# Local attention without values: probabilities times the layer's input, value and output weights folded on the chip

## The reference

```python
def attn_layer(x, Wqkv, qs, ksc, Wo):            # 16 heads of 64
    q, k, v = jnp.split(x @ Wqkv, 3, -1)          # each reshaped to (b, heads, n, 64)
    q = l2norm(q) * qs;  k = l2norm(k) * ksc
    q, k = rotary(q), rotary(k)
    out = local_attention(q, k, v)                # windows of 32 queries, 64 keys: own and previous window
    return out.reshape(b, n, 1024) @ Wo

for i in range(6):
    x = attn_layer(shift_tokens(x), Wqkv[i], q_scale[i], k_scale[i], Wo[i]) + x
    x = ffn_layer(shift_tokens(x), ln_g[i], ln_b[i], W1[i], b1[i], W2[i], b2[i]) + x
```

## Time and profile before

| | |
|---|---|
| time, median of 3 runs | 4451.77 us (4450.44 to 4455.33) |
| time of the profiled execution | 4455.55 us |
| its span | 4454.2 us |
| the last phase in it (from about 1399 us) | some 3055 us |
| one layer (2562 to 3065 us) | 503 us; PE busy 495.2, ACT 414.7, DVE 401.5, POOL 364.6 |
| PE busy over the span | 3995.9 us (90%) |
| chain that ended last, by engine | PE 72%, issue 8%, DVE 7%, POOL 6%, ACT 5% |
| DMA engines' mean busy share in the last phase | 0.25 |
| issues: 128 KB transfers, 64 KB transfers, 63.5 KB, 0.2 KB | 768, 864, 96, 96 |

### The profile page before, as it was taken

The page is one execution under the profiler, slowest core; times in us unless marked ns, Lnnn a source line. Parts: engine busy times, 40 slices in busy tenths (PEclk is TensorE's granted clock), DMA queues, the critical chain, the costliest instruction groups (busy, mean ns, idle before and its releaser), DMA issues.

```text
span 4454.2 us, 182201 instructions
## 1 busy us (share of the span) xinstructions
PE 3995.9 (90%) x79168; PEld 2929.8 (66%) x79168; DVE 3362.1 (75%) x6090; ACT 3370.5 (76%) x5129; POOL 2877.6 (65%) x2623
## 2 busy tenths in 40 slices
PE   7888456666887999999999999999999999999998
PEld 5666345455664667777777767777777767777777
DVE  4665898983555878787888877787888877887875
ACT  4665788884454878888888888887888888888886
POOL 1111788882435877776777777777777777777774
PEclk9999787878998999999999999999999999999999
DMA  2000000000000222222222222222222222222222
GB/s 63 2 2 2 1 1 1 1 1 28 2 2 8 61 66 57 70 64 56 64 67 66 62 61 59 71 62 57 62 59 73 63 58 60 70 66 56 62 56 64
DMA packets 173226, 201.21 MB, mean 45 GB/s; under 512 B 82256, under 2 KB 93712, under 8 KB 172304
## 3 DMA queue, kind: packets, MB, share of 16 engines
q1 hardware_dynamic: 172432, 189.56, 16.8%
HBM read 23.79 MB, written 2.10 MB: 6 GB/s over the span
## 4 chain that ended last, share of the span: by engine, by line
PE 72%; issue 8%; DVE 7%; POOL 6%; ACT 5%; DMA 0%; POOLq 0%; DVEq 0%; ACTq 0%; SPq 0%
PE ps L1331 8%; PE ps L1267 8%; PE ps L1340 7%; PE ps L1268 7%; PE ps L1297 6%; PE ps L1276 5%; PE ps L1315 4%; PE ps L1316 3%; PE ps L1370 3%; PE ps L1364 3%; PE ps L1381 3%; PE ps L1308 2%; DVE arena L616 2%; PE ps L362 2%; PE ps L1287 1%
## 5 line engine op out<-in xcount | busy, mean ns | idle before, releaser
L1605 POOL TENSOR_TENSOR arena<-arena 128x1024 f32<-128x1024 f32 x384 | 722.9, 1904 | 346.9 <-ACT arena L1415 346.9
L1599 POOL TENSOR_TENSOR arena<-arena 128x1024 f32<-128x1024 f32 x384 | 902.1, 2371 | 7.2 <-DVE arena L1507 7.2
L1506 DVE TENSOR_TENSOR arena<-ps,arena 128x1024 f32<-128x1024 f32 x384 | 466.7, 1215 | 189.4 <-ACT arena L1399 183.1
L1618 POOL TENSOR_TENSOR arena<-arena 128x1024 f32<-128x1024 f32 x192 | 365.5, 1904 | 310.3 <-DVE arena L1535 310.3
L1331 PEld LDWEIGHTS ps<-arena 64*64 64x64 f32 x24576 | 381.3, 135 | 166.4 <-issue 165.8
L226 POOL TENSOR_SCALAR arena<-arena 128x2 f32<-128x2 f32 x256 | 73.9, 288 | 611.7 <-DVE arena L220 600.6
L1507 DVE TENSOR_TENSOR arena<-ps,arena 128x1024 f32<-128x1024 f32 x384 | 465.8, 1213 | 0.0
L1515 DVE TENSOR_REDUCE arena<-arena 128x32 f32<-128x2048 f32 x192 | 437.8, 2280 | 0.7 <-issue 0.7
L1267 PE MATMUL ps<-arena 128*128 128x512 f32 x768 | 427.8, 639 | 5.6 <-DVE arena L1507 2.8
L1340 PEld LDWEIGHTS ps<-arena 128*128 128x128 f32 x3072 | 373.0, 192 | 90.4 <-issue 90.1
L1331 PE MATMUL ps<-arena 64*64 64x32 f32 x24576 | 406.1, 220 | 19.9 <-issue 18.9
(11 more groups left out here) (252 smaller groups left out, 9460.6 us busy)
## 6 DMA issues: line engine op xcount, KB each, us to landing
arena<-arena SPq DMA_DIRECT2D x768, 128.0 KB
arena<-arena SPq DMA_DIRECT2D x864, 64.0 KB
arena<-in_dWqkv SPq DMA_DIRECT2D x18, 512.0 KB, 4.9
arena<-arena SPq DMA_DIRECT2D x96, 63.5 KB
arena<-in_dWo SPq DMA_DIRECT2D x6, 512.0 KB
arena<-in_x SPq DMA_DIRECT2D x4, 512.0 KB, 7.5
out<-arena SPq DMA_DIRECT2D x8, 256.0 KB, 2.3
arena<-in_dW SPq DMA_DIRECT2D x6, 341.0 KB, 2.9
```

The lines of the kernel that those rows point to most:

```text
L1506: dve.tensor_tensor(o1, p.rearrange("p (h e) -> p h e", h=16), bc(cs, 1, 16), ALU.mult)
L1599: pool.tensor_tensor(a1[:, half], a1[:, half], T2[:, half], ALU.add).then_inc(*radd[g].up())
L1605: pool.tensor_tensor(a3, a3, bc(ss[:, 16 * g:16 * g + 16], 2, 64), ALU.mult).then_inc(*nrm[g].up())
```

## The change

By associativity, probabilities x (x Wv) x Wo = (probabilities x x) x (Wv Wo). The change computes the product of value and output weights per head on the chip, once a layer (pieces `wv0`, `wv1` on TensorE, `we0`, `we1` on ScalarE, result WVO), and multiplies the probabilities of every head by the layer's shifted input itself:

- Gone per tile: `v`, `vn`, `vd` (8 transfers), `o`, `oT`.
- New per batch: `xd`, 22 transfers on SP out of XX into XW (two buffers), the stretches of the input that the windows need. xd of batch m waits, among others, for u0 and u1 of tile 2m-3, the last readers of its buffer.
- New per tile: `u0` and `u1` (4 matmuls of 64 rows x 128 outputs x 256 columns each, the two row halves into different PSUM banks), `uT0`, `uT1` (two copies of 128 x 1024). u0, u1 wait for xd of their batch.
- `wo` has 16 steps of 128 x 128 in place of 8, and waits for both uT.
- The table of numbers is another one, so all pieces stand in a new order, and PSUM slots are handed out anew; the weights' loads change accordingly (wvT and wo for the next layer early, at 8000). XS has three buffers in place of four.

```diff
-    TILE = {"q1": 999, "q0": 1401, ..., "o": 7478, "oT": 8280, "wo": 9611, "xxa": 10157}
-    BATCH = {"sh": 0, "xs": 598, "fd": 12837, "fst": 15069, "frs": 17286, "fn": 18737, ...
+    TILE = {..., "ex": 7311, "pn": 7674, "sum": 7840, "PT": 8499,
+            "p": 8653, "uT1": 8779, "u1": 8911, "uT0": 9719, "u0": 9883, "xxa": 10114, "wo": 10515}
+    BATCH = {"xs": 0, "sh": 362, "xd": 6011, "fd": 12295, "frs": 12295, "fst": 12701, "fn": 18195, ...
...
-            if piece == "o":
...
+            if piece in ("u0", "u1"):
+                g = int(piece[1])
                 pe.wait_ge(*S.PT.at(n + 1))
+                pe.wait_ge(*xw[m % 2].at(352 * (m // 2 + 1)))
+                p, pT, w = claim(piece, n), PT[n % 2].rearrange("p (g c b q) -> p g c b q", g=2, c=8, b=2), XW[m % 2]
+                for blk in range(2):
+                    for u in range(2):
+                        half = slice(64 * u, 64 * u + 64)
+                        i = pe.matmul(p[:, 512 * u:512 * u + 512].rearrange("p (c b q) -> p c b q", c=8, b=2)[:, :, blk, :],
+                                      w[half, k % 2, 2 * g + blk, :], pT[half, g, :, blk, :], start=True, stop=True,
+                                      skip_group_check=True)
+                i.then_inc(*u_ps[g].up())
             if piece == "wo":
...
+                for u in range(2):
+                    for c in range(8):
+                        i = pe.matmul(p[:, 0:128], o[:, u, c, :], w[:, u, c, :], start=(u == c == 0), stop=(u == 1 and c == 7))
...
-            if piece == "vd":
...
+            if piece == "xd":
+                m = l * NB + k
+                if m == 0:
+                    sp.wait_ge(*S.zeroed.at(1))
+                if l:
+                    sp.wait_ge(*S.xxf.at(m - NB + 1))
+                if m >= 2:
+                    sp.wait_ge(*S.u0_ps.at(2 * m - 2))
+                    sp.wait_ge(*S.u1_ps.at(2 * m - 2))
+                x, got = XX[:, 2 * k:2 * k + 2, :], xw[m % 2]
+                for u in range(2):
+                    w = XW[m % 2][64 * u:64 * u + 64]
+                    sp.dma_start(w[0:32, 1, 0, 0:64], x[96:128, 0, 0:64]).then_inc(*got.dma())
+                    sp.dma_start(w[0:33, 1, 0, 64:128], x[95:128, 0, 64:128]).then_inc(*got.dma())
+                    sp.dma_start(w[0:1, 1, 1, 64:128], x[127:128, 0, 64:128]).then_inc(*got.dma())
+                    sp.dma_start(w[32:64, :, 0, 0:64], x[0:32, :, 0:64]).then_inc(*got.dma())
+                    sp.dma_start(w[33:64, :, 0, 64:128], x[0:31, :, 64:128]).then_inc(*got.dma())
...
```

More of the change, by code:

```diff
@@ L1213, in phase_d @@
     PP = [sb([128, 16, 64]) for _ in range(3)]
-    VN = [sb([128, 1024]) for _ in range(3)]
-    VW = [sb([128, 3, 512]) for _ in range(2)]
+    XW = [sb([128, 2, 4, 128]) for _ in range(2)]
+    WVO = [sb([128, 2, 8, 128]) for _ in range(2)]
     PT = [sb([128, 1024]) for _ in range(2)]
-    OT = [sb([128, 8, 128]) for _ in range(2)]
+    UT = [sb([128, 2, 8, 128]) for _ in range(2)]
     SM = [sb([128, 3, 16]) for _ in range(3)]
     FB = [(stats(C), sb([128, 2]), sb([128, 2, 128]), sb([128, 2, 128]), sb([128, 3, 256])) for _ in range(NF)]
-    TILE = {"q1": 999, "q0": 1401, "sq1": 1620, "ro1": 1906, "ro0": 1925, "sq0": 1965, "ssum": 2373, "radd1": 2611,
[3 rows of a table removed]
[L1225 to L1228, removed]
+    TILE = {"sq1": 1943, "ro1": 2031, "ro0": 2073, "sq0": 2108, "q1": 2140, "q0": 2147, "radd1": 2171, "radd0": 2343,
[3 rows of a table added]
+    BATCH = {"xs": 0, "sh": 362, "xd": 6011, "fd": 12295, "frs": 12295, "fst": 12701, "fn": 18195, "fzT": 18325,
+             "ft": 18600, "fge": 23416, "fg": 23491, "fgm": 24153, "fa": 24480, "xxf": 28268, "fo": 28542}
+    LAYER = {"tab": 16000, "lvo": 8000, "wv0": 15650, "wv1": 15651, "we0": 16496, "we1": 16497,
+             "lqk": 33247, "lln": 48375, "lw1": 54580, "lb1": 54203, "lw2": 58742}
+    EDGE = {"e0": 30168, "e1": 31268, "e2": 33168, "e3": 33218, "out": 35568}
     order = [(1000 * (NT * l + k) + t, piece, l, k) for piece, t in TILE.items() for l in range(depth) for k in range(NT)]
@@ L1231, in phase_d @@
     order += [(1000 * NT * l + t, piece, l + 1, 0) for piece, t in LAYER.items() for l in range(depth - 1)]
+    order += [(-4000 + n, piece, 0, 0) for n, piece in enumerate(("wv0", "wv1", "we0", "we1"))]
     end0 = 1000 * NT * (depth - 1)
@@ L1246, in phase_d @@
             bufs.take((piece, l * NB + k), 1000 * (l * NT + 2 * k) + BATCH[frees[piece]])
+        if piece in ("wv0", "wv1"):
+            bufs.take((piece, l), 1000 * NT * (l - 1) + LAYER["we" + piece[2]] if l else -1000)
     def ps(what, n):
@@ L1265, in tile @@
                     pe.wait_ge(*ld_qk[g].at(16 * l + 16))
[L1266 removed]
+                p, w = claim(piece, n), wqk[:, 1024 * g:1024 * g + 1024]
                 pe.matmul(p[:, 0:512], xs, w[:, 0:512], start=True, stop=True)
@@ L1310, in tile @@
                 i.then_inc(*S.p_ps.up())
[L1311 to L1316, removed]
-            if piece == "o":
-                pe.wait_ge(*S.PT.at(n + 1))
[L1319 to L1333, removed]
@@ new lines, in tile @@
+            if piece == "wo":
+                for g in range(2):
+                    pe.wait_ge(*uT[g].at(n + 1))
+                    if k == 0:
+                        pe.wait_ge(*we[g].at(l + 1))
+                p, o, w = claim("wo", n), UT[n % 2], WVO[l % 2]
+                for u in range(2):
+                    for c in range(8):
+                        i = pe.matmul(p[:, 0:128], o[:, u, c, :], w[:, u, c, :], start=(u == c == 0), stop=(u == 1 and c == 7))
+                i.then_inc(*S.wo_ps.up())
@@ new lines, in fold @@
+        def fold(piece, l):
+            g = int(piece[2])
+            if g == 0:
+                pe.wait_ge(*L.ld_vo.at(32 * l + 32))
+            p = claim(piece, l)
+            for c in range(4):
+                for u in range(2):
+                    half = slice(64 * u, 64 * u + 64)
+                    i = pe.matmul(p[:, 512 * u + 128 * c:512 * u + 128 * c + 128], wvT[half, 4 * g + c, :], wo[half, 4 * g + c, :],
+                                  start=True, stop=True, skip_group_check=True)
+            i.then_inc(*wv_ps[g].up())
@@ L1385, in pe_program @@
         for piece, l, k in order:
+            if piece in ("wv0", "wv1"):
+                fold(piece, l)
             if piece in TILE:
@@ L1476, in act_program @@
         for piece, l, k in order:
+            if piece in ("we0", "we1"):
+                folded(piece, l)
             if piece in TILE:
@@ L1629, in spread @@
             pool.tensor_scalar(nb, nb, -1.0, None, ALU.mult).then_inc(*S.frs.up())
+        for w in XW:
+            pool.memset(w[:, 0, 0:2, :], 0.0)
         for s in XS:
```

118 lines of the change are left out of this document (55 added, 63 removed), and 5 rows, old and new, of the table TILE.

## The result

The changed kernel takes 6429.52 us (median of 4 runs, 6426.05 to 6433.13) where the kernel before took 4453.55 beside it: 1.4431 times as long, 95% interval 1.4413 to 1.4448. The forecast was 6350, range 5900 to 6950.

What follows compares the result with a forecast made beforehand. TensorE bounded the kernel before, at 31.4 us a batch; after, a closed loop through SP's queue would take 51.5 us a turn. 1596 + 92 x 51.5 = 6334, plus some 16 us for a drain: 6350 us, range 5900 to 6950.

Steps and rivals of the forecast that it cites:

- The loop: u0, 22 xd issues, fd, fst, sum, mx, back to u0 through SP's and VectorE's orders: 51.5 us a turn; chance 0.84.
- fst, sum, mx: VectorE's part of the turn, from fd's landing until mx frees the PSUM slot wo claims: 4.8 us.
- wo, mask and s0: TensorE's pieces after its stop: wo 3.56, mask with s0 1.00, and +2 us for the fallen clock.
- p of 2B+5 to the end of u0: TensorE's pieces of the turn, in its order, up to u0 of tile 2B+5: 18.5 us.
- 22 issues: SP issuing the 22 xd transfers of a batch at 0.64 us each, something added for long ones: 15.0 us a turn.
- The upper end, 19.3: High case for SP's xd issues: the two single-row transfers each take 2.73 us, so 19.3 us in place of 15.0.
- fd's landing: From fd's issue on SP to the start of fst on VectorE: 6.3 us a turn.
- the fold ... early and off the path: nothing: 16 small matmuls and two copies per layer, some 3 us of work six times, claimed to cost nothing.
- -0.04 us: nothing: TensorE's work per tile: v and o gone, wo longer, u0 and u1 new; sum -0.04 us.
- A rival: Loop not closed, fd gets out in time, TensorE bounds as before: about 4445 us, 4400 to 4520; chance 0.05.
- The estimate worked out from the Trainium skill: Each 31-row transfer in xd holds SP 0.7 us more, two a batch, 1.4 us a turn; turn 52.9 with it.

Runs made afterwards that it cites:

- (1): Changed kernel with xd at 6311 in place of 6011, so SP issues fd ahead of xd: 4523.65 us, 1.0144 times the kernel before.
- (3): Changed kernel without the second half of xd, 11 transfers per batch in place of 22: 5747.56 us (one run).
- (6): Changed kernel with fd's 127-row transfer cut into one of 64 rows and one of 63: 6243.63 us (one run).
- (2): Changed kernel with fst and frs about one tile later in the orders of VectorE and GpSimd, SP's order unchanged: 5251.09 us (one run).
- experiment 5: Changed kernel with the fold's places altered so each half takes one PSUM slot and is done before the next: 6355.03 us (one run).
- Experiment 7: Changed kernel with fd ahead of xd and the fold on one PSUM slot at a time: 4440.53 us, 0.9967 times the kernel before.

## Why the prediction was right

The loop was closed, as forecast, and its terms came out so (predicted, then the turn from 3000.61 to 3051.74):
- fst, sum, mx: 4.8, measured 4.65.
- wo, mask and s0: 4.6 and 2 for the clock, 6.6 in all; measured 6.66 (a median of 6.59 over the turns). The granted clock was 0.50 (the 1.2 GHz level) in the stretch from 3001 to 3005, in which TensorE stood still, and 0.62 in the five us after; wo took 5.66 us there and 3.57 in the same turn at 1.00.
- p of 2B+5 to the end of u0: 18.5, measured 17.77. Here three sizes were off in one direction: the three u pieces take 2.86 and not 3.15, fa 1.30 and not 1.49, t1 0.49 and not 0.64.
- 22 issues: 15.0, measured 15.77. The upper end, 19.3 (15.0 + 2 x 2.1 is 19.2), rested on the single rows taking 2.73 as in the earlier trace rows; they take 0.52 here (L1718). What holds the one row of fd isn't that it is small, but the 127 rows ahead of it.
- fd's landing: 6.3, measured 6.28. Sum 51.13, against 51.5. That it is so close is partly luck: 0.7 us too much for TensorE and 0.8 too little for the issues cancel.

That the loop and not TensorE's work made the time is shown from three sides: open it (1), shorten its transfers (3), shorten its landing (6); the last two moved the total by somewhat less than 92 times the piece, 682 us of 750 and 186 of 214, and wo, slower in both, makes up part of it. Where a turn closes depends on the orders of VectorE and of the PSUM slots as well (2).

Two things were off. The five long turns, 85 us together above the median, weren't foreseen: "the fold ... early and off the path: nothing" counted its matmuls and copies, and not the PSUM slots it holds. Without them experiment 5 ended at 6355, so they make 74 of the 79 us from 6350 to 6429. And "-0.04 us: nothing" for TensorE's work was too dear. With the loop open a batch takes 29.5 us and not 31.1. The pair u0 and u1 takes 1.92 us, not 2.10. t1 takes 0.49 behind u1, a piece of the same 64 rows and 128 columns, where it took 0.64 behind another shape, and fa and fg 1.30 in place of 1.49. t0 takes 0.50 in place of 0.64 too, but p, which now stands ahead of it, takes 0.64 in place of 0.50, so that exchange gives nothing. This is 0.36 + 0.30 + 0.38, about 1.0 of the 1.5 us a batch; the rest I can't place piece by piece. A rival said 4445 for the loop not closed. Experiment 7 is that case, at 4440.53, but not for the rival's reason: its batches are 1.5 us shorter and its ten long ones take most of that back, so the match is luck.

The estimate worked out from the Trainium skill (the same section of DMA: Bandwidth & Descriptors), 0.7 us more for each issue behind a 31-row transfer, did not show: L1720 carries 31 rows, and the issue behind it (L1721) takes 0.65 us, as L1723 does elsewhere with the same 64 rows. That section of the Trainium skill gives the number of queues of a transfer. That the next issue then waits, in proportion to the runs, was my own step: the wait behind 127 rows is there (experiment 6), the one behind 31 isn't.

## What to carry to other kernels

A transfer that must wait for a buffer holds every transfer behind it in its queue, with all its own issues (0.5 to 0.9 us each on SP here); whenever an edit gives transfers a reuse wait (a wait until the last readers of their buffer are done), follow what stands behind them until you come back to what they wait for, through engine orders and PSUM slots as well as data. If the way closes within one batch, its length is the new period, unless the busiest engine needs longer anyway. Before judging such a change, repair the order: here one number gave back 1906 us, and only then could be seen what the new arithmetic is worth. Price a small side job not only by its work but also by the slots it keeps from others.

## What the runs showed of the hardware

- SP's time for one issue in the kernel after depends on its rows (medians): 32 rows 0.58 us (L1716; 0.60 the second time through), 33 rows 0.85 (L1717), 64 rows in two parts 0.61 to 0.66, 31 rows in two parts 0.72, 63 rows 0.85 (L1722), 127 rows 0.73 and then 2.74 for the next one. The 33 and 63 rows are dearer than the 32, the 64 and the 31.
- The row halves of TensorE run two at a time also in fp32 matmuls of 64 by 256: the passes of u start in pairs, the second a median of 7 ns after the first and the next pair 226 ns later, 16 passes in 1.92 us, 120 ns a pass; a pass of fa with 128 rows takes 1.30 / 6 = 217 ns.
- A group of 16 transposes takes 0.64 us in the chain behind a piece of another tile shape and 0.50 behind one of the same: p and t0 here (0.64, 0.50), t and p before (0.64, 0.50 in the earlier trace rows). That the change of shape is the cause wasn't tested by itself.
- TensorE's work right behind its stop wasn't faster where the stop was shorter: after a median stop of 19.8 us (the kernel after), 17.5 (experiment 6) and 11.7 (experiment 3), wo to the end of s0 took a median of 6.59, 6.95 and 7.25 us, at a mean granted clock of 0.71, 0.70 and 0.64. Full speed is 1.00, and wo alone takes 3.57 us there.
